# Up chunks 0 and 1 by seven products in the last two of four token blocks, with another order at the head, in an MLP kernel on one core

## Time and profile before

| | us |
|---|---|
| median of 3 runs | 2334.75 (2334.61 to 2336.58) |
| the profiled execution, whole | 2335.83 |
| its span | 2333.7 |
| PE busy | 2317.7 (99% of the span) |
| DVE busy | 1634.8 (70%) |
| ACT busy | 1086.9 (47%) |
| POOL busy | 829.3 (36%) |
| DMA, mean over the span | 239 GB/s |

### The profile page before, as it was taken

The page is one execution under the profiler, slowest core; times in us unless marked ns, Lnnn a source line. Parts: engine busy times, 40 slices in busy tenths (PEclk is TensorE's granted clock), DMA queues, the critical chain, the costliest instruction groups (busy, mean ns, idle before and its releaser), DMA issues.

```text
span 2333.7 us, 27748 instructions
## 1 busy us (share of the span) xinstructions
PE 2317.7 (99%) x10504; PEld 1927.2 (83%) x10504; DVE 1634.8 (70%) x1810; ACT 1086.9 (47%) x1253; POOL 829.3 (36%) x682
## 2 busy tenths in 40 slices
PE   8999999999999999999999999999999999999999
PEld 6888888888877888888888888888888888888887
DVE  4349999976265989897334598898723568989850
ACT  3247776223233787722124387761213448785110
POOL 5467878796444021123024321304004413030500
PEclk9999999999999999999999999999999999999999
DMA  7798878878898666665778766665667865556555
GB/s 277 280 394 294 292 245 311 293 243 310 287 363 302 206 196 191 204 201 180 234 237 277 249 194 193 195 209 189 207 219 255 279 221 195 193 192 214 180 190 180
DMA packets 191047, 558.43 MB, mean 239 GB/s; under 512 B 20161, under 2 KB 29377, under 8 KB 190913
## 3 DMA queue, kind: packets, MB, share of 16 engines
q1 hardware_dynamic: 190912, 556.65, 71.0%
HBM read 429.62 MB, written 126.94 MB: 238 GB/s over the span
## 4 chain that ended last, share of the span: by engine, by line
PE 93%; DMA 3%; DVE 1%; SPq 1%; POOL 1%; ACT 0%; issue 0%; DVEq 0%; ACTq 0%
PE bank L945 30%; PE bank L947 30%; PE bank L946 30%; PE bank L965 2%; DMA mixed_w<-mixes 1%; DMA split_w<-w 1%; DMA w<-mixed_w 1%; PE bank L956 1%; POOL w L732 0%; SPq L565 0%; SPq L569 0%; PE bank L1038 0%; PE bank L1039 0%; DMA raw<-w_gate_dram 0%; POOL w L735 0%
## 5 line engine op out<-in xcount | busy, mean ns | idle before, releaser
L1292 DVE TENSOR_SCALAR_CACHE_REDUCE junk_v<-mag,cand 128x2816 bf16<-128x2816 f32 x248 | 780.3, 3146 | 8.8
L786 ACT ACTIVATE junk_s<-mag,cand 128x2816 uint8<-128x2816 f32 x248 | 655.4, 2643 | 222.2 <-DVE cand L1284 195.7
L945 PE MATMUL bank<-w,tok 128*128 128x512 f32 (+1 forms) x952 | 365.8, 384 | 1.8 <-DMA w<-split_w 1.7
L947 PE MATMUL bank<-w,tok 128*128 128x512 f32 (+1 forms) x952 | 364.3, 383 | 0.0
L946 PE MATMUL bank<-w,tok 128*128 128x512 f32 (+1 forms) x952 | 364.1, 382 | 0.0
L732 POOL TENSOR_TENSOR w<-raw,w 128x512 fp32r<-128x512 f32 (+1 forms) x196 | 268.1, 1372 | 77.5 <-ACT w L774 67.8
L945 PE MATMUL bank<-w,prod_t 128*128 128x512 f32 x672 | 269.4, 401 | 0.0
L947 PE MATMUL bank<-w,prod_t 128*128 128x512 f32 x672 | 262.8, 391 | 0.0
L946 PE MATMUL bank<-w,prod_t 128*128 128x512 f32 x672 | 261.9, 390 | 0.0
L945 PE MATMUL bank<-tok,w 128*128 128x512 f32 x640 | 249.0, 389 | 0.0
L946 PE MATMUL bank<-tok,w 128*128 128x512 f32 x640 | 249.0, 389 | 0.0
(11 more groups left out here) (149 smaller groups left out, 3728.3 us busy)
## 6 DMA issues: line engine op xcount, KB each, us to landing
w<-split_w SPq DMA_DIRECT2D x516, 512.0 KB, 3.5
split_w<-w SPq DMA_DIRECT2D x192, 512.0 KB, 4.9
w_more<-split_w SPq DMA_DIRECT2D x60, 512.0 KB, 5.2
w<-mixed_w SPq DMA_DIRECT2D x108, 256.0 KB, 3.5
rows<-x_dram SPq DMA_DIRECT2D x32, 512.0 KB, 4.9
raw<-w_down_dram SPq DMA_DIRECT2D x44, 256.0 KB, 3.9
raw<-w_up_dram SPq DMA_DIRECT2D x40, 256.0 KB, 3.1
w<-split_w SPq DMA_DIRECT2D x24, 392.0 KB, 3.5
```

Of the source, the lines that this page charges most:

```text
L786: act.activation(junk_s[:, :, :], mag[:, :, t, :], ACT.Sign, scale=-1.0, bias=cand[:, t:t + 1], accum_out=cnt[:, t:t + 1]).then_inc(counte ...
L945: pe.matmul(out, left[0], right[0], start=first, stop=False)
L947: return pe.matmul(out, left[1], right[0], start=False, stop=last)
L1292: dve.tensor_scalar(junk_v[:, :, :], mag[:, :, t, :], cand[:, t:t + 1], float(1 - (GATED - KEPT)), ALU.is_lt, ALU.add, accum_out=cnt[:, t: ...
```

## The change

Plans are now made per block, with `FAST = [0, 3, 4, 4]` pairs.

- **Fourth pair.** In blocks 2 and 3 up 0 and up 1 are a fourth pair right after the third, granules 92 to 119, with no plain granules of up 0 and up 1 later. Such a block has 260 granules: latent starts at 120, shared 3 ends at 199, up 2 is 200 to 207, up 3 is 208 to 215, the output starts at 216.
- **Spill.** The results of the fourth pair lie where the hidden values will be. At granule 123 SP stores both chunks, 1 MB each, into a DRAM tensor `spilled_u`, and ACT's first read of hidden waits for that. At granule 199 SP loads them back. DVE multiplies in their signs (`sign_up`) in front of the masks of groups 0 and 1, due at granules 205 and 207.
- **Search** in blocks 2 and 3: steps due at granules 101, 108 and 115, among the reads of the fourth pair, and then every 2.75 granules from 122; ties after 199.
- **Sums** S3 and S4 of blocks 2 and 3 move to the space of `acc`, so ACT waits at granule 10 for the outputs of the block before to be stored.
- **Mixes.** In block 1 the loads and stores of the third pair's mixes are spread, one tile of 256 KB per granule number, the first at granules 4 to 7. The fourth pair's four mixes are made in block 1 by POOL (loads from granules 96, 114, 132, 150 on; mixes at 107, 125, 143, 161).
- **Head.** 32 turns of the identity (`WARM`) come first on PE; the weight product is taken slice by slice between the tokens; ACT makes the first high parts ahead of the second token's square root.

The core of the diff:

```
-FAST = len(PAIRS)
+FAST = [0, 3, 4, 4]
+            first = up_end + FAST_LAG + 4
+            steps_at = [first, first + 7, first + 14]
+            steps_at += [last + 3 + (11 * k + 3) // 4 for k in range(BITS + 1 - len(steps_at))]
+        self.back_at = end[("shared", 3)] if FAST[b] > SPILLED_PAIR else None
+        read = {("up", c): self.back_at + 5 + 2 * c for c in range(2)} if self.back_at else {}
+WARM = 32
+FIRST = [("token", 0), ("weights", 0, 0), ("token", 1), ("weights", 0, 1), ("weights", 0, 2), ("weights", 0, 3),
+         ("token", 2), ("weights", 1, 0), ("token", 3), ("weights", 1, 1), ("weights", 1, 2), ("weights", 1, 3)]
-MIX_LOADS = {8: range(8, 10), 32: range(10, 11), 40: range(11, 12)}
+MIX_LOADS = {4: (8, 0), 5: (8, 1), 6: (8, 2), 7: (8, 3), 10: (9, 0), 13: (9, 1), 16: (9, 2), 19: (9, 3),
+             31: (10, 0), 33: (10, 1), 35: (10, 2), 37: (10, 3), 39: (11, 0), 41: (11, 1), 43: (11, 2), 45: (11, 3)}
-MIX_STORES = {26: 8, 34: 9, 46: 10, 54: 11}
+MIX_STORES = {at + 2 * i: (n, i) for n, at in ((8, 21), (9, 29), (10, 44), (11, 52)) for i in range(4)}
+LATE_LOADS = {96 + 18 * n + 2 * i: (LATE_MIXES + n, i) for n in range(HALF) for i in range(4)}
+LATE_AT = {96 + 18 * n + 11: LATE_MIXES + n for n in range(HALF)}
+LATE_STORES = {96 + 18 * n + 14 + i: (LATE_MIXES + n, i) for n in range(HALF) for i in range(4)}
-SUMS_HI_AT = {2: 4, 4: 3}
+SUMS_HI_AT = [{}, {2: 4, 4: 3}, {10: 4, 12: 3}, {10: 4, 12: 3}]
+                if plan.back_at:
+                    if m == plan.fast_end + 4:
+                        spill(b, 1)
+                        spill(b, 0)
+                    if m == plan.back_at:
+                        load_back(b, 0)
+                        load_back(b, 1)
...
             def mask(b, g):
+                if (b, g) in SIGNED and g < 2:
+                    sign_up(b, g)
...
             standard(0, 0)
+            first_parts(0)
             standard(1, 1)
-            first_parts(0)
             first_parts(1)
+            first_parts(2)
             first_tokens(0)
-            first_parts(2)
```

More of the change, by code:

```diff
@@ L110, with __init__ @@
 class Plan:
-    def __init__(self, later):
-        self.later = later
+    def __init__(self, b):
+        later = b > 0
         found = _plain(*_tail) if later else []
-        for p in range(FAST if later else FIRST_PAIRS):
+        for p in range(FAST[b] if later else FIRST_PAIRS):
             found += _fast_pair(p) if later else _first_pair(p)
-        steps = _middle + _last
+        steps = [step for step in _middle + _last if step[0] not in sum(PAIRS[:FAST[b]], ())]
         if not later:
@@ L136, in __init__ @@
                 self.end[g.key] = m
-        self.up0, self.out0, self.out1 = (self.start[key] for key in (("up", 0), ("out", 0), ("out", 1)))
-        end, up0, out0, out1 = self.end, self.up0, self.out0, self.out1
+        self.out0, self.out1 = (self.start[key] for key in (("out", 0), ("out", 1)))
+        end, out0, out1 = self.end, self.out0, self.out1
+        ups = end[("shared", 3)] + 1
         self.read_at = {end[key] + LAG: key for key in end if key[0] in ("gate", "latent", "routed", "shared")}
@@ L150, in __init__ @@
[L150 to L156 removed]
+            self.fast_at.update({last + 2: (FAST[b] - 1, 5), last + 3: (FAST[b] - 1, 6)})
@@ new lines, in __init__ @@
+            self.signs_at = {end["fast", p, q] + FAST_LAG + 3: (p, q) for p in range(UP_PAIR) for q in (5, 6)}
+            up_end = end["fast", UP_PAIR, 6]
+            self.signs_at[last + 4 if up_end == last else up_end + FAST_LAG + 3] = (UP_PAIR, 6)
+        if later and FAST[b] > SPILLED_PAIR:
+            first = up_end + FAST_LAG + 4
+            steps_at = [first, first + 7, first + 14]
+            steps_at += [last + 3 + (11 * k + 3) // 4 for k in range(BITS + 1 - len(steps_at))]
+        else:
+            first = last + 5 if later else end[("gate", GC - 2)] + LAG + 1
+            steps_at = [first + 3 * k for k in range(BITS + 1)]
@@ L161, in __init__ @@
+        read.update({key: end[key] + LAG for key in end})
+        self.mask_at = {max(self.search_end + 1 + i, read.get(("up", g), 0) + 1): g
                         for i, g in enumerate(GROUPS[:-1])}
@@ L180 @@
 TURN_LEAD = 5
-PLANS = [Plan(b > 0) for b in range(BLOCKS)]
+PLANS = [Plan(b) for b in range(BLOCKS)]
 FIRST_PLAN = PLANS[0]
@@ L355, with spills @@
 FAST_SILUS = 4 * (GC - 1)
+SIGNED = [(b, g) for b in range(1, BLOCKS) for g in (GC - 2, 0, 1)[:3 if FAST[b] > SPILLED_PAIR else 1]]
+def spills(b):
+    return sum(n > SPILLED_PAIR for n in FAST[:b + 1])
 MAG_STEPS = (GC - 1) + 4
@@ L425, in program, with sums_of @@
         sums_raw = {i: over(f"sums{i}_raw", [P, HALF, 2 * P], F32, sums_at[i][1]) for i in (1, 2)}
+        sums_acc = {i: [over(f"sums{i}_acc{part}", [P, HALF, 2 * P], F32R, acc_at + 8 * N * (2 * (i - 3) + part))
+                        for part in range(2)] for i in (3, 4)}
+        assert 32 * N == TILES * HID * 4
+        def sums_of(b, i):
+            return sums_acc[i] if i > 2 and FAST[b] > SPILLED_PAIR else sums[i]
         a11 = [over(f"a11_{j}", [P, HALF, P], F32, signs_at + 4 * j * N) for j in range(2)]
@@ L860, in read_step @@
                                 act.wait_ge(mixes_stored[n], 16 * (FIRST_MIXES // 2))
+                        if FAST[b] > SPILLED_PAIR and i == 0 and t == 0:
+                            for c in range(2):
+                                act.wait_ge(spilled[c], 16 * spills(b))
                         act.wait_ge(bank_filled, filled(b, (*name, t)))
@@ L994, in fast_granule @@
                     if left[0] == "S":
-                        parts = [part[:, k, columns] for part in sums[int(left[1])]]
+                        parts = [part[:, k, columns] for part in sums_of(b, int(left[1]))]
                     else:
@@ L1049, in _ @@
             pe.wait_ge(ident_ready, 2)
-            for kind, i in FIRST:
+            for n in range(WARM):
+                pe.transpose(banks[3][:, 0:P], ident[:, :], ident[:, :])
+            for kind, i, *slices in FIRST:
                 if kind == "token":
```

181 lines of the change are left out of this document (118 added, 63 removed).

## The result

The changed kernel took 2340.20 us (median of 20 runs, 2337.28 to 2342.41), the kernel before on the same chip 2336.16 us (20 runs, 2334.61 to 2338.29). The ratio is 1.0017, interval [1.0011, 1.0023]: 4 us slower. I had forecast 2328.0, so the direction was wrong too. The prediction had called a difference under 0.2% one that can't be told from none; this one is 0.17%, and with 20 runs on each side its interval lies above 1. The profiled execution took 2338.45 us with a span of 2336.7, 3.0 more than before. The matmuls did go, 48 of 128x512, and 32 turns came: the page counts 10504 for PE before and 10488 now.

What follows compares the result with a forecast made beforehand. After the head, PE was taken as the bound: number of matmuls by their pace. Terms -10.9 + 8.0 - 3.3 - 0.5 = -6.7 us, taken from the median 2334.75, gave 2328.0; range to hold 8 in 10, 2319 to 2335.

Steps and rivals of the forecast that it cites:

- matmuls removed: Blocks 2 and 3: 24 fewer matmuls each, 48 at 0.2267 us, a gain of 10.9 us.
- DVE in the fourth pair: Blocks 2 and 3: search steps and reads fit before PE needs its banks; 0 lost, bounds 0 to 2 us a block.
- first turned tile: After the search in blocks 2 and 3: PE waits 4.0 us each for DVE's read of up 2; 8.0 lost.
- pairs of block 1: Spreading the mix loads cuts PE's waits of 4.3 us with restarts to 1 us; gain 3.3 us (0 to 4.3).
- head: Start of the kernel: the second first_copy starts some 0.5 us sooner; gain 0.5 us (-0.3 to 1.0).
- ACT's waits: Search after the fourth pair: six places where ACT also has reads stretch the steps by 10 us (bounds 7 and 14.5).
- step 30: Search step before the masks: starts at 1570.5 on block 2's clock, against 1576.3 before.
- Step 3: First search step after the fourth pair: starts at 1368.1, with latent beginning on PE at 1366.9.
- Rival 4: The pair does not pay: DVE late by 2 us in the fourth pair, 4.0 at the turn; 2332 us, chance 0.10.
- Rival 1: The masks are not late: no wait at the first turned tile; 2320 us, chance 0.23.
- Rival 3: Slower: every sign and mask runs beside POOL, the first turn waits 10 us a block; 2340 us, chance 0.06.
- rival 2: The waits of block 1 stay, the DMA queues being the limit, not the burst; 2331.3 us, chance 0.14.

Runs made afterwards that it cites:

- experiments 7: The changed kernel with the head as before (no turns, old order of weights, tokens and high parts): 2336.05 us, a single run.
- experiment 8: The changed kernel without the 32 turns at the head, its new order kept: 2336.15 us, a single run.
- experiment 2: The changed kernel with the third pair's mixes in block 1 loaded and stored as before: 2337.83 us, ratio 1.0009 to the kernel before.
- experiment 5: The changed kernel with third search step at granule 120, third pair's mixes as before, up 2 read before group 1's mask: 2327.84 us, ratio 0.9968.
- experiment 6: As experiment 5, but block 1's mixes 8 and 9 loaded one tile every second granule: 2325.66 us, ratio 0.9957 to the kernel before.
- experiment 1: The changed kernel with the third search step of blocks 2 and 3 at granule 120 instead of 115: 2336.67 us, ratio 1.0006.

## Why the prediction was wrong, step by step

| term | forecast | in the profile after |
|---|---|---|
| matmuls removed | -10.9 | -10.9 |
| DVE in the fourth pair | 0 | +9.7 (5.6 and 4.1) |
| first turned tile | +8.0 | +1.3 (0.67 and 0.64) |
| pairs of block 1 | -3.3 | +3.2 |
| head | -0.5 | +0.1 |
| sum | -6.7 | +3.4 (spans: +3.0) |

- **Matmuls.** Right: the same pace and 48 less. (The working gives the fourth pair as 37 us in one place and as 38.1, which is right, in another; nothing hangs on it.)
- **DVE and ACT in the fourth pair: the step that failed most.** I wrote "Spare 1.7 us at the closest place: I take 0, with 0 to 2 us a block as the bounds". The closest place was the right one, T4's low part. Without POOL beside it the layout holds: it is ready 30.2 us after the third pair (1362.59 + 0.64 - 1333.0), where I had 30.9. With POOL's low parts, which I had read for PE's sake only, DVE lost 5.6 us. I had priced what POOL does to DVE at the masks and not here, where a sign of the same kind meets POOL's low parts. The loss, 5.6 and 4.1 us, was over twice the bound of 2 a block: waits of 2.86 and 2.66 us, and in block 2 the lower clock behind the first.
- **The first turned tile.** Mis-sized: 0.67 in place of 4.0 a block. Two errors went against each other. The search was done sooner: ACT's waits were 4.6 us where I took 10 (bounds 7 and 14.5), and step 30 began 199.6 us after latent in place of 203.6. From the first mask to up 2's first bank it took 25.2 us, and I had 24.4: the signs took 2.28 each, not 4.4 and 4.9, but the mask of group 1 took 6.75 and not 3.5, and those of groups 4, 5 and 0 took 11.0 and not 8.5. That the last two misses nearly cancel the first is luck. (Step 3 itself began 1.2 us after latent, as I had it.) The place was right: with the third step moved there the wait became 2.5.
- **Block 1.** Wrong in sign. The spreading did remove the weight load's wait, as I said, put one of 1.47 us for a low part of POOL's beside it, and made mix 10's last tile late, in front of reads that PE waits for. I asked what the burst did to the weight loads, not which engine stood waiting for the last tile of a mix. The trace had the place: one wait of the earlier trace rows was already for DVE's `mag`, of 0.31 us.
- **Head.** The first gate granule came 2.3 us sooner, not 0.5. The new order alone moved it by nothing on the other chip (38.14 and 38.21 in experiments 7 and 8); what moved it here is the clock, which the turns did raise. I had not followed the gain through block 0. There the chain of waits before and after runs over stores and loads of split weights and mixes of 5 to 8 us each, not over PE; by 143 us all was gone.
- **Rivals.** Rival 4 had the place (DVE late in the fourth pair), at 2 us a block, 4 in all, where it was 9.7. Rival 1 was near at the first turn (0.5 us of wait) and 20 us off in the time. Rival 3, the slower one, had the sign and the wrong mechanism. No rival had block 1's loss; rival 2 only had that it would gain nothing. The prediction gave 0.05 to slower and 0.32 to a difference too small to tell; the ratio, 0.17%, lies just under its line of 0.2% between the two, the median just above its 2339.4. Either way too little was put on this side of the kernel before, with 1.7 and 2.6 us to spare in DVE's queue at places where a loss turns into a wait of PE and then into the lower clock.

The median rose by 4.0 us and the profiled span by 3.0. The runs of the changed kernel whose mean granted clock was 0.996 took 2341.9 to 2342.4 us, those at 0.999 took 2337.3 and 2338.7. Stretches at the lower clock come behind some long waits and not behind others of the same length and place (2.64 us in experiment 2 without, 2.64 in experiment 8 with). That they make this spread is likely and was not tried.

## What to carry to other kernels

When work moves into a stretch, list what GpSimd does there: the sign test, absolute value, signs and settles of VectorE, when they met a GpSimd instruction, were held until it ended, whatever their own length, while counts and reads out of PSUM were not. So for the kinds that are held count meetings and not sizes. Behind a spread load, look for the instruction that waits for its last piece, and for what stands behind it in that engine's queue; a read that frees a PSUM bank should stand in front of both. A cut of matmuls pays only as far as these reads keep up: with the same 48 matmuls out the kernel took 4 us more, then 7.5 us less than before, after three orders of DVE and SP had changed.

## What the hardware showed that I had not expected

- A VectorE instruction of four columns took 1.27 us beside GpSimd, 0.17 alone, and the block acts both ways: a GpSimd product of 256 columns took 2.82 us beside a sign of 2.28 us that had begun 0.06 us before it, and 1.19 at the same place in the kernel before.
- 32 turns of the identity from 2.02 to 8.14 us were followed, after a wait of 2.15 us, by products at the full clock from the first on. In experiment 5 the wait was 3.25 us; the first products were 0.23 apart, and from 12.77 us on they were 0.43 apart. In experiment 6 it was 2.91, and they were 0.43 apart from 12.99 us on; in experiment 1 it was 2.92, and they stayed at 0.23.
- Over the ten profiles, PE had 18 waits of 2.2 to 4.3 us in the body; behind 13 of them 4 to 13 matmuls lay 0.43 us apart, up to 2.6 us on top of the wait. Behind the 16 waits of 1.0 to 1.7 us none did.
